# Mixture-of-experts stage: weighted inputs from transposed activations and spread routing weights, in place of transposes of weighted inputs

## The chip, the cores and the metric

The kernel runs on one core of a Trainium2 chip. The metric is the device time of one launch in microseconds. The five instruction streams of the core that matter here are PE (TensorE, matrix multiplies), DVE (VectorE), ACT (ScalarE), POOL (GpSimd) and SP (which here only issues DMAs).

## The reference

Sixteen sequences of 256 tokens with 128 channels pass through four blocks, each followed by a layer norm: a state-space block, a mixture of experts, a second state-space block, and a transformer of six layers. All data are float32. The change is in the mixture of experts only:

```
def _moe_linear(x, router_w, expert_w):      # 8 experts, top 2
    logits = x @ router_w.T
    vals, idx = top_k(logits, 2)
    combine = sum over k of softmax(vals)[k] * onehot(idx[k])    # [tokens, 8]
    return sum over e of combine[:, e:e+1] * (x @ expert_w[e].T)
g = _moe_linear(x, router_gate, w_gate)      # 128 -> 512
u = _moe_linear(x, router_up,   w_up)        # 128 -> 512
d = _moe_linear(silu(g) * u, router_down, w_down)   # 512 -> 128
```

`combine` has two nonzero entries in a row, but the kernel computes all eight experts for every token and multiplies by the weights. For `g` and `u` it puts the weight on the input: `combine[t, e] * x[t, :]` is made first, for 8 experts of `g` and 8 of `u`, and the eight products are summed in PSUM.

## The kernel before

The work is four phases, one after another: `ssm_phase`, `moe_phase`, `ssm2_phase`, `transformer_phase`. `X` (all sequences, tokens on partitions, in two halves `t` of 128) stays in SBUF between them.

`moe_phase` (L489) runs 17 passes written out in a loop (`passes`, L535). Pass n does the routing part R of sequence n beside the expert part M of sequence m = n-1. The order on each engine is the order of the code; there is no planner, and semaphores alone tie the engines together (`Steps` counts the steps of a sequence on each engine).

- **PE**, in a pass (L716 to L730): `r_xt` transposes x of sequence n (two 128x128 blocks); `m_experts(0, ..)` is the gate product of sequence m (L689, 4 column chunks of 8 experts, into `pg`); `r_lg` the router logits; `m_experts(1, ..)` the up product into `pu`; between its four chunks, `r_ct` transposes the 16 weighted inputs `xc` of sequence n (two blocks each, 32 transposes, L672); `m_ld` the logits of the down router; `m_down(0)` and `m_down(1)` the down product (L713).
- **DVE**: the top-2 of sequence n (`top2`, L544), the 32 products x times weight into `xc` (L584, tokens on partitions, so that a weight is one value a partition), then for sequence m `it` = silu(g) * u (L590), the second top-2, the weighted sums of the down product (L600, eight for each half t), and the layer norm.
- **ACT**: the copy of the transposed x to `xT` (L620), exponentials, silu of `pg` (L629), and 16 copies of the transposed weighted inputs from PSUM to `xcT` (L633), which the gate and up products of the next pass read. `xcT` has two buffers.
- **POOL and SP** do nothing in this phase. All loads of the phase's weights were issued in the phase before (L133).

Waits that matter: `r_ct` waits for `xc` (L668) and, from the third on, for ACT's copy two before (L670), because there are two PSUM banks for it; `m_ld` waits for `it` and for ACT's last copy (L697, L699), since it writes the same bank; the gate product waits for all copies of its sequence (L682).

Of the kernel before, what the change touches and what calls it, by code (L numbers as in the profile page):

```python
# [20 lines left out]
ALU = mybir.AluOpType  # L21
# [467 lines left out]
def moe_phase(nc, I, X, ident, experts):  # L489
# [3 lines left out]
    with ctx:  # L493
        wg, wu, wd = experts.wg, experts.wu, experts.wd
        rgu, rd, iota = experts.rgu, experts.rd, experts.iota
        xT = sb("b_xT", [P, L])
        lg = sb("b_lg", [P, 3 * T, NE])
        mx = sb("b_mx", [P, 3 * T, 8])
        ix = sb("b_ix", [P, 3 * T, 8], U32)
# [5 lines left out]
        oh = sb("b_oh", [P, 3 * T, NE])  # L505
        o2 = sb("b_o2", [P, 3 * T, NE])
        cb = sb("b_cb", [P, 3 * T, NE])
        xc = sb("b_xc", [P, T, 2 * NE, D])
        xcT = [sb(f"b_xcT{i}", [P, 2 * NE, L]) for i in range(2)]
        sig = sb("b_sig", [P, CF * L])  # L510
        it = sb("b_it", [P, CF, L])
# [12 lines left out]
        loaded, LOADS = experts.loaded, experts.LOADS  # L524

        route = "mx*{0} ix*{0} xf df sm p0 p1 oh*{0} o2*{0} cb"
        pr_ = Steps(ctx, nc, "b_pe_r", f"xt lg ct*{2 * NE}")
        vr = Steps(ctx, nc, "b_dve_r", "lc " + route.format(2 * T) + f" xc*{T * 2 * NE}")
        ar = Steps(ctx, nc, "b_act_r", f"xT ex ctc*{2 * NE}")
        pm_ = Steps(ctx, nc, "b_pe_m", "g*2 u ld d0 d1")  # L530
        vm = Steps(ctx, nc, "b_dve_m", "gu lc " + route.format(T) + f" acc0*{NE} acc1*{NE} bn*2 ag*2 ve nw*{VRS} out*2")
        am_ = Steps(ctx, nc, "b_act_m", "sig*2 ex")
# [2 lines left out]
        def passes(run, eng):  # L535

            for n in range(NSEQ + 1):
                run((n, n % 2) if n < NSEQ else None, (n - 1, (n - 1) % 2) if n else None)

        @block.vector  # L540
        def _(e):
            e.wait_ge(loaded, 16 * LOADS)

            def top2(st, act, n, a, b):  # L544
# [26 lines left out]
                e.tensor_tensor(cb[:, a:b, :], oh[:, a:b, :], o2[:, a:b, :], ALU.add).then_inc(st.sem, 1)  # L571
                e.wait_ge(st.sem, st.at("cb", n))

            def run(R, M):
                if R:
                    n, p = R
                    e.wait_ge(pr_.sem, pr_.at("lg", n))
                    e.tensor_copy(lg[:, 0:2 * T, :], pm[1][:, 0:2 * T * NE].rearrange("p (j n) -> p j n", n=NE))\
                        .then_inc(vr.sem, 1)
                    top2(vr, ar, n, 0, 2 * T)  # L580
                    for x in range(2 * NE):
                        for t in range(T):
                            j = 2 * t + x // NE
                            e.tensor_scalar(xc[:, t, x, :], X[:, n, t, :], cb[:, j, x % NE:x % NE + 1],  # L584
                                            None, ALU.mult).then_inc(vr.sem, 1)
                if M:
                    m, p = M
                    e.wait_ge(am_.sem, am_.at("sig", m))
                    e.wait_ge(pm_.sem, pm_.at("u", m))
                    e.tensor_tensor(it[:, :, :].rearrange("p c l -> p (c l)"), pu[:, :], sig[:, :], ALU.mult).then_inc(vm.sem, 1)  # L590
                    e.wait_ge(pm_.sem, pm_.at("ld", m))
                    e.tensor_copy(lg[:, 2 * T:3 * T, :], pm[1][:, 0:T * NE].rearrange("p (j n) -> p j n", n=NE))\
                        .then_inc(vm.sem, 1)
                    top2(vm, am_, m, 2 * T, 3 * T)
                    for t in range(T):
                        e.wait_ge(pm_.sem, pm_.at(f"d{t}", m))
                        for x in range(NE):
                            if x:
                                e.wait_ge(vm.sem, vm.at(f"acc{t}", m, NE - x))
                            e.scalar_tensor_tensor(acc[:, t, :], pdown[t][:, x * D:(x + 1) * D], cb[:, 2 * T + t, x:x + 1],  # L600
                                                   acc[:, t, :] if x else X[:, m, t, :],
                                                   ALU.mult, ALU.add).then_inc(vm.sem, 1)
                    e.wait_ge(vm.sem, vm.at("acc1", m))
                    layernorm_stats(e, vm, m, lambda t: acc[:, t, :], stats, mv, "")
                    e.wait_ge(vm.sem, vm.at("ag", m))
                    e.tensor_scalar(ve[:, :], mv[:, :, 1], EPS, None, ALU.add).then_inc(vm.sem, 1)
                    vector_rsqrt(e, vm, m, "nw", y[:, :], ve[:, :], h[:, :], tt[:, :])
                    e.wait_ge(vm.sem, vm.at("nw", m))
                    for t in range(T):
                        e.tensor_scalar(X[:, m, t, :], acc[:, t, :], mv[:, t, 0:1], y[:, t:t + 1], ALU.subtract, ALU.mult)\  # L610
                            .then_inc(vm.sem, 1)
            passes(run, e)

        @block.scalar
        def _(e):
            def run(R, M):
                if R:
                    n, p = R
                    e.wait_ge(pr_.sem, pr_.at("xt", n))
                    e.activation(xT[:, :], pm[0][:, 0:L], ACT.Copy).then_inc(ar.sem, 1)  # L620
                    e.wait_ge(vr.sem, vr.at("df", n))
                    e.activation(ex[:, 0:2 * T], df[:, 0:2 * T], ACT.Exp).then_inc(ar.sem, 1)
                if M:
                    m, q = M
                    for j in range(2):
                        e.wait_ge(pm_.sem, pm_.at("g", m, 1 - j))
                        if j == 0 and later(m):
                            e.wait_ge(vm.sem, vm.at("gu", m - 1))
                        e.activation(sig[:, j * 512:(j + 1) * 512], pg[:, j * 512:(j + 1) * 512], ACT.Silu).then_inc(am_.sem, 1)  # L629
                if R:  # L630
                    for x in range(2 * NE):
                        e.wait_ge(pr_.sem, pr_.at("ct", n, 2 * NE - 1 - x))
                        e.activation(xcT[p][:, x, :], pm[x % 2][:, 0:L], ACT.Copy).then_inc(ar.sem, 1)  # L633
                if M:
                    e.wait_ge(vm.sem, vm.at("df", m))
                    e.activation(ex[:, 2 * T:3 * T], df[:, 2 * T:3 * T], ACT.Exp).then_inc(am_.sem, 1)
            passes(run, e)

        @block.tensor
        def _(e):  # L640
            e.wait_ge(loaded, 16 * LOADS)

            def run(R, M):
# [9 lines left out]
                def r_lg():  # L653
                    if R:
                        n, p = R
                        e.wait_ge(ar.sem, ar.at("xT", n))
                        if n >= 2:
                            e.wait_ge(vm.sem, vm.at("lc", n - 2))
                        for t in range(T):
                            m = e.matmul(pm[1][:, t * 2 * NE:(t + 1) * 2 * NE], xT[:, t * P:(t + 1) * P], rgu[:, :],  # L660
                                         start=True, stop=True)
                        m.then_inc(pr_.sem, 1)

                def r_ct(a, b):
                    if R:
                        n, p = R
                        for x in range(a, b):
                            e.wait_ge(vr.sem, vr.at("xc", n, T * (2 * NE - 1 - x)))  # L668
                            if x >= 2:
                                e.wait_ge(ar.sem, ar.at("ctc", n, 2 * NE + 1 - x))  # L670
                            for t in range(T):
                                m = e.transpose(pm[x % 2][:, t * P:(t + 1) * P], xc[:, t, x, :], ident[:, :])  # L672
                            m.then_inc(pr_.sem, 1)

                def m_experts(r, a, b):

                    if M:
                        m, p = M
                        w, o = ((wg, pg), (wu, pu))[r]
                        if a == 0:  # L680
                            if r == 0:
                                e.wait_ge(ar.sem, ar.at("ctc", m))  # L682
                                if later(m):
                                    e.wait_ge(vm.sem, vm.at("acc0", m - 1))
                            elif later(m):
                                e.wait_ge(vm.sem, vm.at("gu", m - 1))
                        for j in range(a, b):
                            for x in range(NE):
                                last = e.matmul(o[:, j * L:(j + 1) * L], w[:, x, j * P:(j + 1) * P], xcT[p][:, r * NE + x, :],  # L689
# [4 lines left out]
                def m_ld():  # L694
                    if M:
                        m, p = M
                        e.wait_ge(vm.sem, vm.at("gu", m))  # L697
                        if R:
                            e.wait_ge(ar.sem, ar.at("ctc", R[0]))  # L699
                        for t in range(T):  # L700
                            for j in range(CF):
                                last = e.matmul(pm[1][:, t * NE:(t + 1) * NE], it[:, j, t * P:(t + 1) * P], rd[:, j, :],
                                                start=j == 0, stop=j == CF - 1)
                        last.then_inc(pm_.sem, 1)
# [9 lines left out]
                                                wd[:, j, b * 512:(b + 1) * 512], start=j == 0, stop=j == CF - 1)  # L714
                        last.then_inc(pm_.sem, 1)
                r_xt()  # L716
                m_experts(0, 0, 2)
                r_lg()
                m_experts(0, 2, 4)
                m_experts(1, 0, 1)  # L720
                r_ct(0, 4)
                m_experts(1, 1, 2)
                r_ct(4, 8)
                m_experts(1, 2, 3)
                r_ct(8, 12)
                m_experts(1, 3, 4)
                r_ct(12, 16)
                m_ld()
                m_down(0)
                m_down(1)  # L730
# [1046 lines left out]
```

## Time and profile before

| | us |
|---|---|
| median of 3 runs (4464.75 to 4467.26) | 4465.24 |
| profiled execution, its own time | 4472.1 |
| its span, first to last instruction | 4470.2 |
| mixed passes of the expert phase, 110.09 to 896.01 | 785.92 |
| one of them (268.42 to 318.93) | 50.51 |

The span is the distance from the first to the last instruction on the core; the profiled execution's own time is 1.9 us longer. The granted TensorE clock is a share of 2.4 GHz, 0.97 over the whole span. "Idle before" in brackets is how long the engine had nothing to do before that instruction, and what it was waiting for.

### The profile page before, as it was taken

Reading aid. Unit: us, or ns where it says so; the run is one execution under the profiler, and the core shown is the slowest. Engines: PE = TensorE matmul, PEld = TensorE weight load, DVE = VectorE, ACT = ScalarE, POOL = GpSimd, SP = SyncE. Lnnn points to the kernel's source line nnn. Section 1 sums busy time; section 2 is a strip of 40 time slices with the busy share of each in tenths; the row PEclk is TensorE's granted clock in tenths of the full one; section 3 lists DMA queues with packets and bytes.
Section 4 is the critical chain, followed back from the end, with each engine's and each line's share of the span. In section 5 each row is a group of like instructions: output and inputs, shape, how many; then the busy total and the mean of one; then the engine's idle time right before and its main releaser. Section 6 shows DMA issues by size and latency. Waiting matters only on the chain.

```text
span 4470.2 us, 146512 instructions
## 1 busy us (share of the span) xinstructions
PE 4226.6 (95%) x64231; PEld 3077.6 (69%) x64231; DVE 3363.1 (75%) x7591; ACT 2458.3 (55%) x4522; POOL 2133.5 (48%) x1317
## 2 busy tenths in 40 slices
PE   5999999988699999999999999999999999998997
PEld 3777776666377777777777777777777777766665
DVE  5444444444698898888988888888888889887784
ACT  2111111111367676776776776767767767666663
POOL 1000000001466666666666666666666666665552
PEclk8999999999799999999999999999999999999998
DMA  3000000000011111111111111111111111111110
GB/s 128 1 1 1 1 1 1 1 1 1 23 40 39 34 50 54 39 36 39 53 50 35 40 39 48 50 39 39 42 51 45 39 34 49 54 37 37 34 34 24
DMA packets 70594, 152.46 MB, mean 34 GB/s; under 512 B 14524, under 2 KB 43079, under 8 KB 69575
## 3 DMA queue, kind: packets, MB, share of 16 engines
q1 hardware_dynamic: 69958, 143.09, 10.8%
q8 instruction: 509, 8.34, 0.8%
q14 instruction: 127, 1.03, 0.1%
HBM read 27.69 MB, written 2.10 MB: 7 GB/s over the span
## 4 chain that ended last, share of the span: by engine, by line
PE 63%; DVE 4%; ACT 3%; issue 3%; POOL 2%; POOLq 0%; DVEq 0%
PE pQ L1537 14%; PE pS L1521 9%; PE pM L1603 7%; PE pO L1581 6%; PE pM L1592 6%; PE pC L1637 5%; PE pO L1568 4%; PE pT L1568 4%; PE pT L1549 3%; PE pC L1647 3%; ACT sq L1406 2%; POOL rot L1166 1%; POOL rot L1174 1%; ACT pS L1390 1%; DVE rot L1256 1%
## 5 line engine op out<-in xcount | busy, mean ns | idle before, releaser
L1174 POOL TENSOR_TENSOR rot<-rot,m 128x1024 f32<-128x1024 f32 x384 | 905.1, 2357 | 397.3 <-DVE m L1260 397.3
L1166 POOL TENSOR_TENSOR rot<-rot,rn 128x1024 f32<-128x1024 f32 x384 | 732.8, 1908 | 245.9 <-DVE rn L102 245.9
L1406 ACT ACTIVATE sq<-pQ 128x1024 f32<-128x1024 f32 x384 | 393.7, 1025 | 463.1 <-PE pQ L1537 463.1
L1183 POOL TENSOR_TENSOR E<-E,rc 128x512 f32<-128x512 f32 x384 | 400.5, 1043 | 352.4 <-DVE rc L1246 352.1
L1256 DVE TENSOR_TENSOR rot<-pQ,tabl 128x1024 f32<-128x1024 f32 x384 | 461.8, 1203 | 36.0 <-ACT sq L1406 35.4
L1568 PEld LDWEIGHTS pO<-PT,V 64*64 64x64 f32 x12288 | 389.9, 135 | 132.8 <-issue 124.1
L1521 PEld LDWEIGHTS pS<-kT,qT 64*32 64x32 f32 x24576 | 369.6, 108 | 141.3 <-issue 105.3
L1260 DVE TENSOR_TENSOR m<-pQ,tabl 128x1024 f32<-128x1024 f32 x384 | 466.2, 1214 | 0.0
L1271 DVE TENSOR_REDUCE n<-sq 128x16 f32<-128x1024 f32 x384 | 464.1, 1209 | 0.0
L1568 PE MATMUL pO<-PT,V 64*64 64x32 f32 x12288 | 432.0, 221 | 29.7 <-issue 27.3
L1521 PE MATMUL pS<-kT,qT 64*32 64x64 f32 x24576 | 434.6, 220 | 22.9 <-issue 12.6
L1592 PE MATMUL pM<-ident,rot 128*128 128x128 f32 x3072 | 422.2, 281 | 23.8 <-POOL rot L1166 23.8
L786 POOL MEMSET c_xn<- 128x48 f32 x1 | 0.1, 147 | 926.6 <-POOLq L493 926.6
L1568 PE MATMUL pT<-PT,V 64*64 64x32 f32 x12288 | 434.7, 221 | 0.0
L1537 PE MATMUL pQ<-wq,xs 128*128 128x512 f32 x768 | 385.9, 625 | 10.5 <-DVE m L1260 9.1
L1568 PEld LDWEIGHTS pT<-PT,V 64*64 64x64 f32 x12288 | 392.1, 133 | 0.0
L1537 PE MATMUL pQ<-wk,xs 128*128 128x512 f32 x768 | 364.9, 598 | 9.0 <-DVE m L1260 9.0
L1592 PEld LDWEIGHTS pM<-ident,rot 128*128 128x128 f32 x3072 | 337.5, 142 | 46.3 <-POOL rot L1166 29.3
L1603 PE MATMUL pM<-wv,xs 128*128 128x512 f32 x768 | 365.1, 598 | 0.0
L1581 PE MATMUL pO<-oT,wo 128*128 128x256 f32 x1536 | 348.6, 380 | 0.6 <-ACT oT L1421 0.4
L1232 DVE TENSOR_REDUCE mx<-pS 128x8 f32<-128x512 f32 x384 | 262.7, 684 | 82.8 <-PE pS L1521 82.6
L1581 PEld LDWEIGHTS pO<-oT,wo 128*128 128x128 f32 x1536 | 285.1, 191 | 36.6 <-ACT oT L1421 1.2
(221 smaller groups left out, 7842.2 us busy)
## 6 DMA issues: line engine op xcount, KB each, us to landing
V<-V SPq DMA_DIRECT2D x192, 384.0 KB, 3.5
xs<-XT SPq DMA_DIRECT2D x192, 64.0 KB, 2.9
V<-V SPq DMA_DIRECT2D x96, 128.0 KB, 3.3
ys<-XT SPq DMA_DIRECT2D x192, 64.0 KB, 2.1
wq<-in_wqkv SPq DMA_DIRECT2D x6, 512.0 KB, 4.8
wk<-in_wqkv SPq DMA_DIRECT2D x6, 512.0 KB, 4.0
wv<-in_wqkv SPq DMA_DIRECT2D x6, 512.0 KB, 5.5
wo<-in_wo SPq DMA_DIRECT2D x6, 512.0 KB, 3.9
```

The costliest lines, as they stand in the source:

```text
L1166: e.tensor_tensor(r, r, rn[b % 2][:, c:c + HEADS].unsqueeze(2).to_broadcast([P, HEADS, HD]), ALU.mult)\
L1174: e.tensor_tensor(rot[j % RING][:, :], rot[j % RING][:, :], m2[:, :, :].rearrange("p h d -> p (h d)"), ALU.add)\
L1256: e.tensor_tensor(rot[j % RING][:, :].rearrange("p (h d) -> p h d", d=HD), pQ[:, :].rearrange("p (h d) -> p h d", d=HD), tl[:, t, 2 * w, : ...
L1260: e.tensor_tensor(m2[:, :, :].rearrange("p h (b d) -> p h b d", b=2), pQ[:, :].rearrange("p (h b d) -> p h b d", b=2, d=HD // 2)[:, :, ::- ...
L1271: e.tensor_reduce(n2[:, c:c + HEADS], sq[:, :].rearrange("p (h d) -> p h d", d=HD), AX.X, ALU.add)\
L1406: e.activation(sq[:, :], pQ[:, :], ACT.Square).then_inc(a_sq.sem, 1)
L1521: x = e.matmul(pS[32 * j:32 * j + 32, b * KEYS:(b + 1) * KEYS], q[r:r + HD, h // 2, WIN * w:WIN * (w + 1)], k[r:r + HD, h // 2, WIN * w:WI ...
L1537: x = e.matmul(pQ[:, i * 512:(i + 1) * 512], xs[n % 3][:, t * P:(t + 1) * P], wqkv[w][:, i * 512:(i + 1) * 512], start=True, stop=True)
L1568: x = e.matmul(pOV[b % 2][c:c + HD, j // 2, w // 4, WIN * (w % 2):WIN * (w % 2 + 1)], V[n % 2][r:r + KEYS, w // 4, 1 - w % 2, h * HD:(h + ...
L1581: x = e.matmul(pO[:, 0:L], wo[:, c, :], oT[:, c, :], start=c == 0, stop=c == N // P - 1)
L1592: x = e.transpose(pM[i][:, c * P:(c + 1) * P], rot[j % RING][:, (4 * i + c) * P:(4 * i + c + 1) * P], ident[:, :])
L1603: e.matmul(pM[i][:, :], xs[n % 3][:, t * P:(t + 1) * P], wqkv[2][:, i * 512:(i + 1) * 512], start=True, stop=True)\
```

## The change

The weighted inputs are made directly in the transposed layout (channels on partitions, tokens along the row). There a weight varies along the row, so that it has to be present on all 128 partitions.

- PE transposes the routing weights `cb` of the two token halves (two transposes, output 16 partitions x 256) in place of the 32 transposes of `xc`. `r_ct` takes its only place between the up chunks 1 and 2; `r_lg` moves ahead by one gate chunk. `m_ld` no longer waits for ACT's copies of sequence n.
- ACT copies that result once to `cT` (16 partitions, a row is one expert's weights over 256 tokens) in place of 16 copies.
- SP, for each of the 16 rows, issues a DMA that reads this row of 1 KB from its one partition of `cT` and writes it to all 128 partitions of `cB` (128 KB written a DMA, 2 MB a sequence). `cB` has one buffer: the DMAs wait for both of its readers of the sequence before.
- DVE multiplies `cB[:, 0:8]` by `xT` in one instruction of 128 x 2048 (step `xg`, gate half), after the sums of half 0 of sequence m; the 32 products at L584 are gone.
- POOL multiplies `cB[:, 8:16]` by `xT` in one instruction of the same size (step `xu`, up half).
- The gate product waits for `xg`, the up product for `xu`. `xT` has two buffers.

```diff
-        xT = sb("b_xT", [P, L])
+        xT = [sb(f"b_xT{i}", [P, L]) for i in range(2)]
+        cT = sb("b_cT", [2 * NE, L])
+        cB = sb("b_cB", [P, 2 * NE, L])
...
-        xc = sb("b_xc", [P, T, 2 * NE, D])
...
+        @block.sync
+        def _(e):
+            for n in range(NSEQ):
+                e.wait_ge(ar.sem, ar.at("ctc", n))
+                if n:
+                    e.wait_ge(vr.sem, vr.at("xg", n - 1))
+                    e.wait_ge(gr.sem, gr.at("xu", n - 1))
+                for x in range(2 * NE):
+                    e.dma_start(cB[:, x, :], cT[x:x + 1, :].unsqueeze(1).to_broadcast([1, P, L])).then_inc(wide[x // NE], 16)
+
+        @block.gpsimd
+        def _(e):
+            for n in range(NSEQ):
+                p = n % 2
+                if n >= 2:
+                    e.wait_ge(pm_.sem, pm_.at("u", n - 2))
+                e.wait_ge(ar.sem, ar.at("xT", n))
+                e.wait_ge(wide[1], 16 * NE * (n + 1))
+                e.tensor_tensor(xcT[p][:, NE:2 * NE, :], cB[:, NE:2 * NE, :], xT[p][:, :].unsqueeze(1).to_broadcast([P, NE, L]), ALU.mult)\
+                    .then_inc(gr.sem, 1)
...
-                    for x in range(2 * NE):
-                        for t in range(T):
-                            j = 2 * t + x // NE
-                            e.tensor_scalar(xc[:, t, x, :], X[:, n, t, :], cb[:, j, x % NE:x % NE + 1],
-                                            None, ALU.mult).then_inc(vr.sem, 1)
...
+                    summed(m, 0)
+                if R:
+                    n, p = R
+                    e.wait_ge(wide[0], 16 * NE * (n + 1))
+                    e.tensor_tensor(xcT[p][:, 0:NE, :], cB[:, 0:NE, :], xT[p][:, :].unsqueeze(1).to_broadcast([P, NE, L]), ALU.mult)\
+                        .then_inc(vr.sem, 1)
+                if M:
+                    summed(m, 1)
...
-                    for x in range(2 * NE):
-                        e.wait_ge(pr_.sem, pr_.at("ct", n, 2 * NE - 1 - x))
-                        e.activation(xcT[p][:, x, :], pm[x % 2][:, 0:L], ACT.Copy).then_inc(ar.sem, 1)
+                    e.wait_ge(pr_.sem, pr_.at("ct", n))
+                    if n:
+                        e.wait_ge(vr.sem, vr.at("xg", n - 1))
+                        e.wait_ge(gr.sem, gr.at("xu", n - 1))
+                    e.activation(cT[:, :], pm[0][0:2 * NE, 0:L], ACT.Copy).then_inc(ar.sem, 1)
...
-                        for x in range(a, b):
-                            e.wait_ge(vr.sem, vr.at("xc", n, T * (2 * NE - 1 - x)))
-                            if x >= 2:
-                                e.wait_ge(ar.sem, ar.at("ctc", n, 2 * NE + 1 - x))
-                            for t in range(T):
-                                m = e.transpose(pm[x % 2][:, t * P:(t + 1) * P], xc[:, t, x, :], ident[:, :])
-                            m.then_inc(pr_.sem, 1)
+                        e.wait_ge(vr.sem, vr.at("cb", n))
+                        for t in range(T):
+                            m = e.transpose(pm[0][0:2 * NE, t * P:(t + 1) * P], cb[:, 2 * t:2 * t + 2, :].rearrange("p j n -> p (j n)"),
+                                            ident[:, :])
+                        m.then_inc(pr_.sem, 1)
...
                             if r == 0:
-                                e.wait_ge(ar.sem, ar.at("ctc", m))
+                                e.wait_ge(vr.sem, vr.at("xg", m))
...
+                                e.wait_ge(gr.sem, gr.at("xu", m))
...
-                        if R:
-                            e.wait_ge(ar.sem, ar.at("ctc", R[0]))
...
                 r_xt()
-                m_experts(0, 0, 2)
+                m_experts(0, 0, 1)
                 r_lg()
-                m_experts(0, 2, 4)
-                m_experts(1, 0, 1)
-                r_ct(0, 4)
-                m_experts(1, 1, 2)
-                r_ct(4, 8)
-                m_experts(1, 2, 3)
-                r_ct(8, 12)
-                m_experts(1, 3, 4)
-                r_ct(12, 16)
+                m_experts(0, 1, 4)
+                m_experts(1, 0, 2)
+                r_ct()
+                m_experts(1, 2, 4)
                 m_ld()
```

## Rows read from the trace of the kernel before

**Rows 1.** The page's second part: the span in 40 slices of 111.8 us
```profile
PE   5999999988699999999999999999999999998997
PEclk8999999999799999999999999999999999999998
GB/s 128 1 1 1 1 1 1 1 1 1 23 40 39 34 50 54 39 36 39 53 50 35 40 39 48 50 39 39 42 51 45 39 34 49 54 37 37 34 34 24
```

**Rows 2.** Timeline of PE, one mixed pass: start, duration, engine, line, [idle before]
```profile
268.42 0.38 PE L650 MATMUL b_pm<-ident,X 128*128 128x128 f32 x2
...
282.90 3.62 PE L689 MATMUL b_pu<-b_xcT,b_wu 128*128 128x256 f32 x16
286.36 0.60 PE L672 MATMUL b_pm<-ident,b_xc 128*128 128x128 f32 x4
287.30 0.69 PE L672 MATMUL b_pm<-ident,b_xc 128*128 128x128 f32 x4 [0.35 <-ACT b_xcT L633]
287.82 3.62 PE L689 MATMUL b_pu<-b_xcT,b_wu 128*128 128x256 f32 x16
...
297.68 3.62 PE L689 MATMUL b_pu<-b_xcT,b_wu 128*128 128x256 f32 x16
301.13 0.60 PE L672 MATMUL b_pm<-ident,b_xc 128*128 128x128 f32 x4
302.08 0.69 PE L672 MATMUL b_pm<-ident,b_xc 128*128 128x128 f32 x4 [0.35 <-ACT b_xcT L633]
303.33 1.92 PE L702 MATMUL b_pm<-b_rd,b_it 128*128 128x8 f32 x16 [0.57 <-ACT b_xcT L633]
305.11 7.11 PE L713 MATMUL b_pg<-b_wd,b_it 128*128 128x512 f32 x16
312.06 7.03 PE L713 MATMUL b_pd<-b_wd,b_it 128*128 128x512 f32 x16
318.93 0.38 PE L650 MATMUL b_pm<-ident,X 128*128 128x128 f32 x2
```

**Rows 3.** Windows, all mixed passes: length, busy by engine, PEclk, DMA share, GB/s
```profile
110.09:896.01 785.92, 756.63 (x3210) 552.80 (x3211) 337.42 (x1653) 148.66 (x346) 0.00 (x0) 0.96 0.00 1
```

**Rows 4.** Timeline of PE, the last pass, which has no routing part
```profile
910.25 13.98 PE L689 MATMUL b_pu<-b_xcT,b_wu 128*128 128x256 f32 x64
925.61 1.95 PE L702 MATMUL b_pm<-b_rd,b_it 128*128 128x8 f32 x16 [1.39 <-DVE b_it L590]
```

**Rows 5.** Timeline of the first pass, which has no expert part
```profile
92.60 0.66 PE L650 MATMUL b_pm<-ident,X 128*128 128x128 f32 x2 [9.19 <-PEq L244]
99.14 0.19 DVE L571 TENSOR_TENSOR b_cb<-b_oh,b_o 128x32 f32<-128x32 f32 x1
99.91 9.71 PE L672 MATMUL b_pm<-ident,b_xc 128*128 128x128 f32 x32 [5.14 <-DVE b_xc L584]
110.09 0.44 PE L650 MATMUL b_pm<-ident,X 128*128 128x128 f32 x2 [0.47 <-ACT b_xcT L633]
```

**Rows 6.** Windows: the loads of the first phase, then a pair of SBUF-to-SBUF copies
```profile
20.00:30.00 10.00, 8.59 (x50) 5.41 (x50) 2.08 (x7) 1.20 (x2) 2.11 (x4) 0.88 0.99 415
2031.25:2033.50 2.25, 2.25 (x14) 1.98 (x13) 2.22 (x3) 1.23 (x1) 1.79 (x1) 1.00 0.78 233
2032.75:2033.50 0.75, 0.75 (x7) 0.69 (x6) 0.72 (x2) 0.00 (x0) 0.75 (x1) 1.00 0.56 202
```

**Rows 7.** Timeline of SP's queue, the issues of those copies (384 and 128 KB)
```profile
2030.23 0.54 SPq L1125 DMA_DIRECT2D V<-V  x1
2030.81 0.60 SPq L1126 DMA_DIRECT2D V<-V  x1
```

**Rows 8.** Groups of instructions: busy us, mean ns of one, idle before
```profile
L1174 POOL TENSOR_TENSOR rot<-rot,m 128x1024 f32<-128x1024 f32 x384 | 905.1, 2357 | 397.3 <-DVE m L1260 397.3
L1183 POOL TENSOR_TENSOR E<-E,rc 128x512 f32<-128x512 f32 x384 | 400.5, 1043 | 352.4 <-DVE rc L1246 352.1
L590 DVE TENSOR_TENSOR b_it<-b_pu,b_sig 128x1024 f32<-128x1024 f32 x16 | 19.6, 1224 | 237.7 <-PE b_pu L689 237.7
```

**Rows 9.** Timeline of PE: the same 32 multiplies after an idle stretch, and warm
```profile
71.34 5.69 PE L465 MATMUL a_pu<-a_xpad,a_fused 128*64 128x256 f32 x32
...
38.81 3.68 PE L465 MATMUL a_pu<-a_xpad,a_fused 128*64 128x256 f32 x32
```

**Rows 10.** Windows around that idle stretch: PEclk is the third number from the end
```profile
70.00:74.00 4.00, 3.81 (x22) 2.45 (x24) 3.00 (x14) 1.43 (x4) 0.00 (x0) 0.50 0.02 4
74.00:78.00 4.00, 3.68 (x30) 2.12 (x26) 2.39 (x6) 0.76 (x3) 0.00 (x0) 0.82 0.00 0
```

**Rows 11.** Timeline of DVE at the end of that mixed pass
```profile
312.34 0.35 DVE L600 SCALAR_TENSOR_TENSOR b_acc<-b_pg,b_cb,X 128x128 f32<-128x128 f32 x1 [3.83 <-PE b_pg L713]
312.73 2.67 DVE L600 SCALAR_TENSOR_TENSOR b_acc<-b_pg,b_cb,b_acc 128x128 f32<-128x128 f32 x7
```

More of the change, by code:

```diff
@@ L526, in moe_phase @@
         route = "mx*{0} ix*{0} xf df sm p0 p1 oh*{0} o2*{0} cb"
-        pr_ = Steps(ctx, nc, "b_pe_r", f"xt lg ct*{2 * NE}")
-        vr = Steps(ctx, nc, "b_dve_r", "lc " + route.format(2 * T) + f" xc*{T * 2 * NE}")
-        ar = Steps(ctx, nc, "b_act_r", f"xT ex ctc*{2 * NE}")
+        pr_ = Steps(ctx, nc, "b_pe_r", "xt lg ct")
+        vr = Steps(ctx, nc, "b_dve_r", "lc " + route.format(2 * T) + " xg")
+        ar = Steps(ctx, nc, "b_act_r", "xT ex ctc")
+        gr = Steps(ctx, nc, "b_pool_r", "xu")
+        wide = [ctx.enter_context(nc.semaphore(f"b_wide_{k}")) for k in "gu"]
         pm_ = Steps(ctx, nc, "b_pe_m", "g*2 u ld d0 d1")
@@ L572, in top2, with summed @@
                 e.wait_ge(st.sem, st.at("cb", n))
+            def summed(m, t):
+                e.wait_ge(pm_.sem, pm_.at(f"d{t}", m))
+                for x in range(NE):
+                    if x:
+                        e.wait_ge(vm.sem, vm.at(f"acc{t}", m, NE - x))
+                    e.scalar_tensor_tensor(acc[:, t, :], pdown[t][:, x * D:(x + 1) * D], cb[:, 2 * T + t, x:x + 1],
+                                           acc[:, t, :] if x else X[:, m, t, :],
+                                           ALU.mult, ALU.add).then_inc(vm.sem, 1)
             def run(R, M):
@@ L594, in run @@
                     top2(vm, am_, m, 2 * T, 3 * T)
-                    for t in range(T):
[L596 to L602, printed above, removed]
+                    summed(m, 0)
[6 more added lines that the diff above has]
+                    summed(m, 1)
                     e.wait_ge(vm.sem, vm.at("acc1", m))
@@ L619, in run @@
                     e.wait_ge(pr_.sem, pr_.at("xt", n))
-                    e.activation(xT[:, :], pm[0][:, 0:L], ACT.Copy).then_inc(ar.sem, 1)
+                    if n >= 2:
+                        e.wait_ge(gr.sem, gr.at("xu", n - 2))
+                    e.activation(xT[p][:, :], pm[0][:, 0:L], ACT.Copy).then_inc(ar.sem, 1)
                     e.wait_ge(vr.sem, vr.at("df", n))
@@ L659, in r_lg, with r_ct @@
                         for t in range(T):
-                            m = e.matmul(pm[1][:, t * 2 * NE:(t + 1) * 2 * NE], xT[:, t * P:(t + 1) * P], rgu[:, :],
+                            m = e.matmul(pm[1][:, t * 2 * NE:(t + 1) * 2 * NE], xT[p][:, t * P:(t + 1) * P], rgu[:, :],
                                          start=True, stop=True)
                         m.then_inc(pr_.sem, 1)
-                def r_ct(a, b):
+                def r_ct():
                     if R:
                         n, p = R
-                        for x in range(a, b):
-                            e.wait_ge(vr.sem, vr.at("xc", n, T * (2 * NE - 1 - x)))
-                            if x >= 2:
-                                e.wait_ge(ar.sem, ar.at("ctc", n, 2 * NE + 1 - x))
-                            for t in range(T):
-                                m = e.transpose(pm[x % 2][:, t * P:(t + 1) * P], xc[:, t, x, :], ident[:, :])
-                            m.then_inc(pr_.sem, 1)
+                        e.wait_ge(vr.sem, vr.at("cb", n))
[3 more added lines that the diff above has]
+                        m.then_inc(pr_.sem, 1)
                 def m_experts(r, a, b):
@@ L681, in m_experts @@
                             if r == 0:
-                                e.wait_ge(ar.sem, ar.at("ctc", m))
+                                e.wait_ge(vr.sem, vr.at("xg", m))
                                 if later(m):
                                     e.wait_ge(vm.sem, vm.at("acc0", m - 1))
-                            elif later(m):
-                                e.wait_ge(vm.sem, vm.at("gu", m - 1))
+                            else:
+                                e.wait_ge(gr.sem, gr.at("xu", m))
+                                if later(m):
+                                    e.wait_ge(vm.sem, vm.at("gu", m - 1))
                         for j in range(a, b):
```

## The prediction, made before the result was known

> **What bounds the kernel now.** I read the slices of the span first, because the change touches one phase. The expert phase begins at 92.6 us and ends near 950, slices 1 to 8; there PE is busy nine tenths or more of nearly every slice, at a clock of nine tenths or more, and the DMA queues move 1 GB/s [rows 1]. So the phase is PE's, with every DMA engine free. The other phases are not touched.
>
> Then the PE timeline of one mixed pass. It lasts 318.93 - 268.42 = 50.51 us, and PE has no gap over 0.6 us in it; the small gaps are at the transposes, where PE waits for ACT's copies [rows 2]. All fifteen mixed passes take 785.92 us, 52.4 each, since in some the granted clock falls for a short stretch (0.96 on average) [rows 3]. Whatever leaves PE's stream in a mixed pass shortens it, until another chain is longer than what is left. That chain is the question here, for the change builds a new one, through SP and the DMA engines, where nothing ran before.
>
> **What is removed.** Each of the three inner groups of 8 transposes costs PE the distance to the next up chunk, 287.82 - 286.36 = 1.46 us (three groups: 4.4) [rows 2]. The fourth is followed by `m_ld`: from the end of the up product (297.68 + 3.62 = 301.30) to the down router at 303.33 are 2.03 us; in the last pass, where no transposes stand there, the same distance is 925.61 - (910.25 + 13.98) = 1.38 us, ended by DVE's `it` [rows 2, 4]. The fourth group is therefore worth only 0.65 us, because `it` is late next. The two new transposes cost about what `r_xt`'s two do, 0.3 us (busy 0.38, partly pipelined) [rows 2]. Net on PE: 4.4 + 0.65 - 0.3 = 4.75 us a mixed pass, 71 us over fifteen. ACT's 16 copies and DVE's 32 products go too; neither engine was the bound, so this earns nothing beyond the gaps counted.
>
> **What is added, in order of the chain for one sequence.**
> - ACT's one copy to `cT`: about 0.4 us. With the two transposes and the hand-overs, 1.1 us from the end of up chunk 1 to `cT` ready.
> - SP issues 16 DMAs. An issue of this kind takes 0.54 to 0.60 us, so 16 take 9 us [rows 7]; the data of the first flow about 1.0 us after issue starts (issue at 2030.23, bytes from 2031.25) [rows 6, 7]. SP has nothing else to do in this phase, so nothing is queued behind.
> - The DMAs move 16 x 131,072 bytes = 2.10 MB. Call their duration D.
> - POOL's `xu`, 128 x 2048. No such row exists; 128 x 512 takes 1.04 us and 128 x 1024 up to 2.36 us [rows 8], so between 4 x 1.04 = 4.2 and 2 x 2.36 = 4.7 us. I take 4.2, and 0.8 for the landing and the semaphores on either side. POOL has no other work, so nothing stands behind its wait.
> - PE's up chunks 0 and 1 (6.9 us at full clock, twice the 3.4 that separate 282.90 from 286.36) [rows 2]. `r_ct` stands behind them in program order, so that the weights of sequence n+1 cannot be transposed before `xu` of sequence n is done. `cB` has one buffer, and its DMAs wait for the same `xu` anyway.
> - DVE's `xg`: 2 x 1.22 = 2.4 us [rows 8]. It stands between the two sums of the down product. Each sum takes 3.0 us (0.35 and 2.67) [rows 11], and the second's input comes 7.0 us after the first's (a down half on PE) [rows 2]. So `xg` is hidden if the gate rows have landed by then; if not, the second sum, the layer norm and the top-2 of the next sequence wait behind it. The gate rows are the first half of D, and PE's next gate product waits for `xg` as well.
>
> The cycle from one `cT` to the next is therefore 1.0 + D + 0.8 + 4.2 + 6.9 + 1.1 = D + 14 us. With D under about 30 us it hides behind the remaining 45.8 us of PE work of a pass. Everything rests on D.
>
> **D.** The trace shows no DMA that reads one partition. All 16 engines together move 415 GB/s when they spread over 128 partitions, 26 GB/s each [rows 6]. The quickest case is that reading one partition 128 times is no slower: 2.10 MB at 415 GB/s are 5 us, at the 233 GB/s of the SBUF-to-SBUF pair 9 us, the same as SP's issues [rows 6, 7]. The slowest is that a partition gives no more than the rows show for one: the end of that pair, L1126, which reads 32 partitions by the code, runs at 202 GB/s, or 6.3 GB/s a partition, which makes D 333 us [rows 6]. In between lies one lane's rate: if all 16 engines have to draw from the one place where the row lies, they share what the trace shows one engine to move, 26 GB/s. A DMA then takes 131,072 / 25.9 GB/s = 5.06 us and D is 81 us. I take this value. In every fast row the bytes go to or from many partitions at once; here sixteen engines want the same 1 KB, row after row, and a source that all of them share has not been seen to give more than one of them takes. It is also the value of the three that lies nearest to a row in kind: a rate of one path, not of all and not of a guess per partition.
>
> The Trainium skill speaks against this change at the same place: by "SBUF — State Buffer", section "Door 1: The DMA port swizzle", DMA bandwidth depends on how many of the 16 SBUF ports a transfer's partitions reach, about 27.2 GB/s a port, with partitions 0 to 3 on one port. By its figure (an estimate) a row would take 4.8 us, D would be 77 us and the time some 64 us below my forecast. Its table speaks of tiles at both ends' width and not of a repeated source row; no row of this trace shows it.
>
> **The sum with D = 81 us.** PE now idles some 25 us a pass before the up product. After such an idle stretch the clock stands at 0.50, the 1.2 GHz level, and comes back within the next window [rows 10]; 32 multiplies that take 3.68 us warm took 5.69 there [rows 9], so 2.0 us more a resumption. The cycle is 81 + 14 + 2 = 97 us. In the first pass `cb` is ready at 99.33; two transposes at the low clock (0.66) and the copy put `cT` at 100.7 [rows 5]. The fifteenth cycle later is 100.7 + 15 x 97 = 1555.7; DMAs and `xu` of sequence 15 add 87, and the last pass's up product starts at 1642.7 in place of 910.25 [rows 4]. With 2 us for the cold start the rest moves by 1642.7 - 910.25 + 2 = +735 us; written for any D, with D + 16 a cycle, it is 15 (D + 16) + D + 6 + 100.7 - 910.25 + 2, or 16 D - 561. Against the profiled execution's own 4472.1 us that is 5207; the runs' median lies 6.9 us lower, so 5200 us.
>
> **The rivals.**
> - *The source row is no bottleneck.* D is 5 to 30 us, the chain hides, and PE keeps the 4.75 us a pass. In the first pass, DVE and PE reach 110 us as before (`cT` at 100.7, 1.0 to the first data, eight issues 4.5, landing 0.8: 107; `xg` 2.4). 4472.1 - 71 = 4401 on the profile, 4394 on the median; 4380 to 4420 with the clock's short falls going either way. For it: idle queues, rows of 1 KB, 16 engines, 415 GB/s seen. Against it: never seen from one partition. It decides from D = 35 us (16 D = 561), 60 GB/s, twice and a third what one engine's share is.
> - *Half a bottleneck.* The rows overlap at two or more places and run at 33 to 60 GB/s: D 35 to 63, time 4465 to 4910. The 16 rows lie on consecutive partitions and the DMAs are started in order, so I see little to spread them.
> - *Worse than one lane.* Sixteen readers in each other's way, or a single partition giving less: 20 GB/s makes D 105 and 5584 us, the 6.3 GB/s above 9230 us.
> - *The change doesn't take PE's transposes away.* Excluded by the diff; they are gone from the stream.
>
> **How the numbers follow.** Forecast (D 63 to 97 us, 4910 to 5450): 0.55. Worse than that: 0.12. Half a bottleneck: 0.06. Source row no bottleneck: 0.25. Landing within 0.2% of before by a D near 35: 0.02. A difference of 0.2% (9 us) is about what a measurement of this kernel can tell from none. So faster 0.25, same 0.02, slower 0.73. The forecast's own range is 4910 to 5450 us. As the fast case has more than 2 in 10, the range must reach it: 4380 to 5450, which leaves the 0.12 above outside.
>
> **What would show it.** Right: SP's queue with 16 issues a pass and the DMA busy share high for some 80 us each time; `xu` starting 83 us after `cT`; PE waiting for POOL before the up product 25 us a pass and for DVE before the gate product; granted clock 0.5 after each; the L672 rows down from 512 to 32; a phase of 1580 us. Wrong: if the rows land within 15 us of issue and PE's pass lasts 46 us, the source row was no bottleneck; if the share is high and D well over 100 us, one partition gives less than one lane.

## The result, and the profile after

| | before | changed |
|---|---|---|
| median of 3 runs, us | 4465.24 | 5042.53 (5038.19 to 5044.11) |
| span of the profiled execution, us | 4470.2 | 5040.7 |
| ratio, 95% interval | | 1.129 (1.1271 to 1.1309) |

The change costs 577 us. The time lies inside the stated range and on the side that was forecast; the forecast itself, 5200, was 158 us too high.

The second part of the page of the changed kernel, in slices of 126 us:

```profile
PE   4565555556567699999999999999999999999997
PEclk7777777778779899999999999999999999999998
DMA  4757565766640011111111111111111111111110
GB/s 119 27 22 27 22 26 23 26 24 24 26 17 1 12 39 36 39 49 49 40 36 47 49 40 40 40 52 41 40 40 52 44 36 40 50 46 39 35 36 23
```

The expert phase now fills slices 1 to 11. PE is busy half of it, where it was busy nine tenths and more [rows 1]; the 16 DMA engines are busy some six tenths of it and yet move only 22 to 27 GB/s in all slices but the last. In the first phase of before, engines with a busy share of 0.99 moved 415 GB/s [rows 6], so here most of the busy time must be waiting inside the transfers.

One pass on PE, and the POOL products of two sequences:

```profile
560.23 0.38 PE L682 MATMUL b_pm<-ident,X 128*128 128x128 f32 x2
574.97 5.99 PE L721 MATMUL b_pg<-b_xcT,b_wg 128*128 128x256 f32 x16 [14.36 <-DVE b_xcT L627]
...
581.17 10.61 PE L721 MATMUL b_pg<-b_xcT,b_wg 128*128 128x256 f32 x48
609.99 9.01 PE L721 MATMUL b_pu<-b_xcT,b_wu 128*128 128x256 f32 x32 [18.21 <-POOL b_xcT L561]
618.84 0.38 PE L701 MATMUL b_pm<-ident,b_cb 128*16 128x128 f32 x2
619.05 7.07 PE L721 MATMUL b_pu<-b_xcT,b_wu 128*128 128x256 f32 x32
627.54 1.95 PE L732 MATMUL b_pm<-b_rd,b_it 128*128 128x8 f32 x16 [1.42 <-DVE b_it L618]
```
```profile
605.44 4.50 POOL L561 TENSOR_TENSOR b_xcT<-b_cB,b_xT 128x2048 f32<-128x2048 f32 x1 [82.73 <-DMA b_cB<-b_cT]
691.81 4.49 POOL L561 TENSOR_TENSOR b_xcT<-b_cB,b_xT 128x2048 f32<-128x2048 f32 x1 [81.88 <-DMA b_cB<-b_cT]
```

PE's 32 transposes are gone, and two long waits stand in their place: 14.4 us for `xg`, DVE's product of weights and inputs for the gate half, and 18.2 us for `xu`, POOL's product for the up half. Both in turn wait for DMAs. A pass lasts 86.4 us here (691.81 - 605.44), 86.8 on average over the phase, in place of 50.5 in the pass shown before and 52.4 on average [rows 2, 3]. The distance from the end of the up product to the down router, ended by `it`, is 1.42 us, close to the 1.39 of the last pass of before [rows 4].

The DMAs by tile, durations in ns of issue (least, median, most) and the time to landing:

```profile
L551 SPq DMA_DIRECT2D b_cB<-b_cT x256: 469/4912/4949, 99.8 to 1458.2; - x128
DMA to landing us min/median/max: 6.9/15.9/17.9
```

An issue took 0.54 to 0.60 us before [rows 7]. Here the median is 4.91 us, and a DMA lands 15.9 us after its issue, so that about three (15.9 / 4.91) are under way at a time. I read this as a full queue: SP can put in a DMA only when one leaves. Then a DMA of 131,072 bytes takes 4.91 us, which is 26.7 GB/s. In one-microsecond windows of the first sequence, with one of 70 us at the end (third to last number: clock; then the busy share of the DMA engines; last: GB/s):

```profile
119.00:120.00 1.00, 0.00 (x0) 0.00 (x0) 0.00 (x0) 0.00 (x0) 0.00 (x0) 0.50 0.81 26
120.00:121.00 1.00, 0.00 (x0) 0.00 (x0) 0.00 (x0) 0.00 (x0) 0.00 (x0) 0.50 0.99 83
121.00:122.00 1.00, 0.00 (x0) 0.00 (x0) 0.00 (x0) 0.00 (x0) 0.00 (x0) 0.50 0.77 25
...
138.00:139.00 1.00, 0.00 (x0) 0.00 (x0) 0.00 (x0) 0.00 (x0) 0.00 (x0) 0.50 0.80 74
139.00:140.00 1.00, 0.00 (x0) 0.00 (x0) 0.84 (x1) 0.00 (x0) 0.00 (x0) 0.50 0.90 29
...
153.00:154.00 1.00, 1.00 (x6) 0.90 (x5) 0.00 (x0) 0.00 (x0) 0.00 (x0) 1.00 0.70 84
...
101.00:171.00 70.00, 16.79 (x68) 14.15 (x68) 6.10 (x28) 2.69 (x4) 0.00 (x0) 0.62 0.81 30
```

The rate stays between 20 and 31 GB/s, except near 120 us, from 133 to 139 us and from 153 to 156 us. Counted at 4.9 us a row from 101, these are the fourth, the eighth and (after what the first two saved) the twelfth row. Something changes every four rows. 2.10 MB take 70 us.

### The profile page after: what moved, and what is told of

It is laid out like the page before. It is cut to its first block, busy times and chain, and to the rows that moved or that the text cites. A ratio compares the mean times of both kernels' runs of the same rounds, so it can differ in the third digit from the quotient of the medians.

```text
span 5040.7 us, 144925 instructions
## 1 busy us (share of the span) xinstructions
PE 4228.1 (84%) x63751; PEld 3072.6 (61%) x63751; DVE 3295.6 (65%) x7095; ACT 2380.3 (47%) x4282; POOL 2207.6 (44%) x1333
## 4 chain that ended last, share of the span: by engine, by line
PE 56%; DVE 3%; issue 3%; ACT 3%; POOL 2%; POOLq 0%; DVEq 0%
PE pQ L1562 13%; PE pS L1546 8%; PE pM L1628 6%; PE pM L1617 6%; PE pO L1606 6%; PE pC L1662 5%; PE pO L1593 4%; PE pT L1593 3%; PE pT L1574 3%; PE pC L1672 2%; ACT sq L1431 2%; POOL rot L1191 1%; POOL rot L1199 1%; DVE rot L1281 1%; ACT pS L1415 1%
## 5 line engine op out<-in xcount | busy, mean ns | idle before, releaser
L561 POOL TENSOR_TENSOR b_xcT<-b_cB,b_xT 128x2048 f32<-128x2048 f32 x16 | 71.9, 4495 | 1383.6 <-DMA b_cB<-b_cT 1383.6
L721 PE MATMUL b_pu<-b_xcT,b_wu 128*128 128x256 f32 x1024 | 264.3, 423 | 297.1 <-POOL b_xcT L561 297.1
L721 PE MATMUL b_pg<-b_xcT,b_wg 128*128 128x256 f32 x1024 | 261.3, 420 | 283.3 <-DVE b_xcT L627 283.3
L618 DVE TENSOR_TENSOR b_it<-b_pu,b_sig 128x1024 f32<-128x1024 f32 x16 | 19.6, 1224 | 654.3 <-PE b_pu L721 654.3
L721 PEld LDWEIGHTS b_pu<-b_xcT,b_wu 128*128 128x128 f32 x1024 | 218.1, 216 | 339.3 <-POOL b_xcT L561 303.6
L721 PEld LDWEIGHTS b_pg<-b_xcT,b_wg 128*128 128x128 f32 x1024 | 215.2, 213 | 322.0 <-DVE b_xcT L627 287.9
## 6 DMA issues: line engine op xcount, KB each, us to landing
b_cB<-b_cT SPq DMA_DIRECT2D x256, 128.0 KB, 15.9
```

## The experiments

Theory A: all engines draw a row from one place of SBUF, that place gives 26 to 27 GB/s, and four adjacent partitions share it. Theory B: a DMA of 128 rows of 1 KB from SBUF to SBUF costs this much whatever it reads. Theory C: the limit is the single partition. The times of the changed kernel, wide source and through HBM are medians of 3, 4 and 4 executions; each of the others is one execution, so that I read no difference of a few microseconds from them. "Landed" is from the first issue of sequence 0 to the start of its POOL product, the cycle is the mean distance of the 16 POOL products.

| kernel | landed, us | cycle, us | time, us |
|---|---|---|---|
| changed | 72.2 | 86.8 | 5042.5 |
| wide source | 11.8 | 46.1 | 4386.0 |
| rows spread | 40.7 | 54.9 | 4530.8 |
| rows in two places | 79.4 | 94.0 | 5153.0 |
| half rows | 36.9 | 49.7 | 4446.5 |
| through HBM | 9.0 | 46.1 | 4387.1 |
| early, two buffers | 72.2 | 66.6 | 4739.1 |
| two queues | 41.0 | 69.3 | 4746.9 |
| order alone | 44.0 | 58.1 | 4578.7 |
| spread and two queues | 30.4 | 49.6 | 4441.3 |

**Wide source.** The same DMAs, with another source. ACT's copy to `xT` besides waits for the `xg` of two sequences before.

```diff
-                    e.dma_start(cB[:, x, :], cT[x:x + 1, :].unsqueeze(1).to_broadcast([1, P, L])).then_inc(wide[x // NE], 16)
+                    e.dma_start(cB[:, x, :], xT[n % 2][:, :]).then_inc(wide[x // NE], 16)
```

> Each of the 16 DMAs reads a tile of 128 partitions (the sequence's transposed activations, xT) in place of one row of cT; size, count, order, targets and waits stay. The spread weights are left out by this, so the weighted inputs are not the reference's. Theory A (all engines draw from one place of SBUF, which gives 26 to 27 GB/s; changed kernel: D of 72 us from the first issue to the POOL product, 87 us a pass): D falls to 9 to 12 us, SP's issues, the chain hides, a pass is 46 us and the time 4380 to 4410 us. Theory B (128 rows of 1 KB between SBUF and SBUF cost 4.4 to 4.9 us a DMA whatever they read): D stays 72 and the time 5040. This run also measures what the removed transposes are worth when the chain is hidden: I said 71 us.

Measured: 4386.04 us, ratio to before 0.9821 (0.9798 to 0.9843). Issues and rate:

```profile
L551 SPq DMA_DIRECT2D b_cB<-b_xT x256: 464/601/1578, 98.2 to 799.0; - x128
```
```profile
100.00:108.00 8.00, 0.82 (x2) 0.73 (x3) 2.29 (x1) 0.00 (x0) 0.00 (x0) 0.50 0.62 207
```

An issue takes 0.60 us again and the rate is 207 GB/s, about SP's pace of one 128 KB DMA every 0.6 us. The targets, sizes and counts are those of the changed kernel, so theory B falls: what costs is what the DMA reads. It also shows that everything else in the change is hidden or gains.

**Rows spread, rows in two places.** Both make a zeroed tile `cw` with DVE copies of the weights at chosen columns, so that the transposes put the rows on chosen partitions; DMA x then reads that partition. In two places, the gate rows lie on 0 to 3 and 32 to 35 and the up rows on 4 to 7 and 36 to 39. The spread layout:

```diff
+                        e.tensor_copy(cw[:, t, :].rearrange("p (j x s) -> p j x s", j=2, s=4)[:, :, 0:NE, 0], cb[:, 2 * t:2 * t + 2, :]).then_inc(vr.sem, 1)
...
-                    e.dma_start(cB[:, x, :], cT[x:x + 1, :].unsqueeze(1).to_broadcast([1, P, L])).then_inc(wide[x // NE], 16)
+                    e.dma_start(cB[:, x, :], cT[64 * (x // NE) + 4 * (x % NE):64 * (x // NE) + 4 * (x % NE) + 1, :].unsqueeze(1).to_broadcast([1, P, L])).then_inc(wide[x // NE], 16)
```

> The 16 rows of cT lie 4 partitions apart: gate rows on partitions 0, 4, ..., 28, up rows on 64, 68, ..., 92 (two DVE copies into a zeroed tile ahead of the two transposes, otherwise the same work). In the changed kernel the rate leaves 26 to 29 GB/s only near rows 4, 8 and 12 (83 GB/s in one microsecond). Theory A, with four adjacent partitions sharing one place: now every row is at a boundary; a row alone takes 4.9 us, 16 take 79, the three boundaries of the changed kernel saved 7, so 2.4 to 2.8 each; 15 of them give D of 36 to 43 us and 4470 to 4590 us. Theory B (cost per DMA): 5040. Theory C (each partition by itself is the limit, so that neighbours already differ): 5040, and the bursts stay near every fourth row.

> The gate rows lie on partitions 0 to 3 and 32 to 35, the up rows on 4 to 7 and 36 to 39; work as in the spread layout otherwise. By the Trainium skill, SBUF — State Buffer, section Door 1, partitions 32 apart are on the same port. If that is so (A with that map) only row 8 is at a boundary: D of 76 us, 5090 to 5120 us, and no burst at rows 4 and 12. If only neighbours share a place (A without that map), bursts at rows 4, 8 and 12 as before and 5040. B and C: 5040.

Measured: spread 4530.8 us, as A expected; in two places 5153.0 us, 33 us above the upper end of A with that map and 110 above the changed kernel. That the one change of place left saved so little there I did not take apart. Windows of the spread kernel, then of the one with two places:

```profile
110.00:120.00 10.00, 0.00 (x0) 0.00 (x0) 0.00 (x0) 0.00 (x0) 0.00 (x0) 0.50 0.82 59
120.00:130.00 10.00, 5.64 (x18) 4.65 (x19) 2.29 (x1) 0.00 (x0) 0.00 (x0) 0.58 0.86 58
```
```profile
120.00:122.00 2.00, 0.00 (x0) 0.00 (x0) 0.00 (x0) 0.00 (x0) 0.00 (x0) 0.50 0.78 25
140.00:142.00 2.00, 0.00 (x0) 0.00 (x0) 0.10 (x1) 0.00 (x0) 0.00 (x0) 0.50 0.82 52
152.00:154.00 2.00, 2.00 (x11) 1.77 (x10) 1.49 (x15) 0.86 (x2) 0.00 (x0) 1.00 0.87 28
```

With each row 4 partitions from the last, the rate is 58 to 59 GB/s from 110 to 130 us. With rows 4 to 7 put 32 partitions above rows 0 to 3, the burst at 120 us is gone, as is the one at the twelfth row; only the one at the eighth, near 140, is left. So the place is shared by four neighbours and, for the partitions tried, by the four that lie 32 above, and theory C falls. The Trainium skill, "SBUF — State Buffer", section "Door 1: The DMA port swizzle", has this map and 27.2 GB/s a port; the traces agree with the map for the partitions tried in this way (0 to 15 and 32 to 39) and, at 26.7 GB/s of reading from one place, nearly with the figure.

**Half rows.**

```diff
-                    e.dma_start(cB[:, x, :], cT[x:x + 1, :].unsqueeze(1).to_broadcast([1, P, L])).then_inc(wide[x // NE], 16)
+                    e.dma_start(cB[:, x, 0:P], cT[x:x + 1, 0:P].unsqueeze(1).to_broadcast([1, P, P])).then_inc(wide[x // NE], 16)
```

> Each DMA moves only the first 128 of 256 tokens of its row (512 bytes to each partition, 64 KB a DMA); the weights of the other tokens are left at zero, so the output differs. 16 DMAs and 128 rows each as before. Theory A: D halves to 36 us, and by 16 us of time for each us of D the time falls by 570 to about 4470 to 4490 us. Theory B, a cost per DMA or per row of it: D stays near 72, time near 5040.

Measured: 4446.5 us, landed in 36.9 us for 72.2. The price goes with the bytes, as A has it, not with the number of DMAs. The time is 24 us below A's range. The cold starts go too, since PE waits 1.4 us or nothing before the up product:

```profile
439.47 7.17 PE L726 MATMUL b_pu<-b_xcT,b_wu 128*128 128x256 f32 x32 [1.43 <-POOL b_xcT L564]
446.48 0.38 PE L706 MATMUL b_pm<-ident,b_cb 128*16 128x128 f32 x2
```

From the start of the up product to the transposes are 7.0 us, where the changed kernel takes 8.85; over fifteen passes that is about 28 us, which A's range had left out.

**Through HBM.** HBM is the memory outside the core; 16 KB go out to it, then two DMAs of 1 MB come in.

```diff
+                e.dma_start(scr[n % 2].rearrange("o x l -> (o x) l"), cT[:, :]).then_inc(staged, 16)
+                e.wait_ge(staged, 16 * (n + 1))
+                for r in range(2):
+                    e.dma_start(cB[:, r * NE:(r + 1) * NE, :], scr[n % 2][:, r * NE:(r + 1) * NE, :].to_broadcast([P, NE, L])).then_inc(wide[r], 16)
```

> SP writes cT (16 KB) to a scratch tensor in HBM, waits for it, and two DMAs of 1 MB spread 8 rows each from there to all partitions. The same result as the changed kernel. Theory A (the limit is the place in SBUF that the row lies in): D is 2 us for the write, 2 to 3 for the first read, 5 to 9 for 2 MB, in all 10 to 14 us; the chain hides and the time is 4380 to 4420 us. Rival (the same bytes read by all engines are slow wherever they lie): D stays at tens of us, time 4600 or more.

Measured: 4387.10 us, ratio to before 0.9827 (0.9811 to 0.9843): 1.7% faster than before, a small gain but clear of the noise, and far faster than the changed kernel, with its computation. It has landed in 9.0 us, a little sooner than the 10 to 14 expected. Its DMAs (KB each, us to landing), the window of sequence 0, and a pass on PE:

```profile
b_cB<-b_scr SPq DMA_DIRECT2D x32, 1024.0 KB, 6.2
b_scr<-b_cT SPq DMA_DIRECT2D x16, 16.0 KB, 1.4
```
```profile
100.00:107.00 7.00, 0.00 (x0) 0.00 (x0) 2.23 (x1) 0.00 (x0) 0.00 (x0) 0.50 0.81 300
```
```profile
438.80 0.38 PE L686 MATMUL b_pm<-ident,X 128*128 128x128 f32 x2
...
460.19 0.38 PE L705 MATMUL b_pm<-ident,b_cb 128*16 128x128 f32 x2
460.40 7.07 PE L725 MATMUL b_pu<-b_xcT,b_wu 128*128 128x256 f32 x32
468.89 1.95 PE L736 MATMUL b_pm<-b_rd,b_it 128*128 128x8 f32 x16 [1.42 <-DVE b_it L622]
...
484.52 0.38 PE L686 MATMUL b_pm<-ident,X 128*128 128x128 f32 x2
```

The same 16 KB are repeated 128 times from HBM at 300 GB/s over 7 us, start included. Count and size of the DMAs differ too from the changed kernel; that these are not the cause rests on the wide source, which kept both. A pass is 484.52 - 438.80 = 45.72 us, 4.79 less than the 50.51 of before [rows 2].

**Early transposes, two buffers.** `cB` and `cT` doubled, and in PE's order:

```diff
-                m_experts(1, 0, 2)
                 r_ct()
-                m_experts(1, 2, 4)
+                m_experts(1, 0, 4)
```

> cB and cT get a second buffer and the two transposes of the weights stand before the up product, so that the DMAs of sequence n+1 no longer wait for the POOL product and two up chunks of sequence n. The DMAs stay as they are. If the cycle is D plus 14 us as predicted, the queue now never runs dry, a pass is 70 to 74 us in place of 87, and the time falls by about 200 to 4800 to 4870 us. Rival (the 14 us were not on the path, or the next transposes are held by the gate rows): no change, 5040.

Measured: 4739.1 us, a cycle of 66.6. So the 14 us were on the path. But the gain is 303 us, not 200, and the time is 61 us below my range. A queue that never runs dry also overlaps the last row of one sequence with the first of the next, which lie in different places. A cycle late in the phase has four bursts about 17 us apart, the fourth at the change of sequence (the POOL product starts at 506.0):

```profile
453.00:454.00 1.00, 1.00 (x7) 0.87 (x6) 0.00 (x0) 0.00 (x0) 0.00 (x0) 1.00 0.67 70
470.00:471.00 1.00, 1.00 (x4) 0.38 (x3) 0.93 (x3) 0.00 (x0) 0.00 (x0) 1.00 0.69 74
487.00:488.00 1.00, 1.00 (x6) 0.90 (x5) 0.63 (x4) 0.05 (x1) 0.00 (x0) 1.00 0.74 95
504.00:505.00 1.00, 0.00 (x0) 0.00 (x0) 0.00 (x0) 0.00 (x0) 0.00 (x0) 0.50 0.64 74
```

2.10 MB in 66.6 us are 31.5 GB/s, against 30 within one sequence of the changed kernel.

**Two queues.** The up rows are issued by ACT after its last exponential of the pass (`for x in range(NE, 2 * NE)` moved there), the gate rows by SP.

> The 8 up rows are issued by ACT on its own queue, after its exponential, while SP issues the 8 gate rows; both read cT as in the changed kernel, at partitions 8 to 15 and 0 to 7. Theory A: two places are read at a time, 50 to 55 GB/s together, D of 40 us and about 4530 us (4470 to 4650; ACT's later work waits behind its issues). Rival D (the engines themselves are held at 26 GB/s in all by this kind of DMA): D stays 72, 5040.

Measured: 4746.9 us, about 100 above A's range; all rows of sequence 0 landed in 41.0 us, as A expected, at 51 to 65 GB/s in windows of 10 us from 110 us on. PE and ACT in a later pass:

```profile
486.76 6.24 PE L725 MATMUL b_pg<-b_xcT,b_wg 128*128 128x256 f32 x16 [19.77 <-DVE b_xcT L627]
...
510.55 0.38 PE L705 MATMUL b_pm<-ident,b_cb 128*16 128x128 f32 x2
```
```profile
442.70 0.37 ACT L665 ACTIVATE b_cT<-b_pm 16x256 f32<-16x256 f32 x1 [6.53 <-PE b_pm L705]
...
454.28 33.42 ACTq L672 DMA_DIRECT2D b_cB<-b_cT  x8
487.81 0.39 ACT L650 ACTIVATE b_xT<-b_pm 128x256 f32<-128x256 f32 x1 [33.33 <-issue]
```

Two places at a time, as A has it, held; my step from D to the time did not. The eight gate rows still take about 39 us from their two places, one after the other (8 x 4.9), and they have a chain of their own: `cT` at 443.07, the gate product from 486.76, then up chunks 0 and 1, the transposes at 510.55 and the next `cT` some 25 us after the start of the gate product, together 68 us. In the changed kernel the up rows' chain (86.8) hid this one. ACT besides sat 33 us in its eight issues, with `xT` behind them.

**Order alone, spread with two queues.** The first is the changed kernel with one line:

```diff
-                for x in range(2 * NE):
+                for x in (0, 4, 1, 5, 2, 6, 3, 7, 8, 12, 9, 13, 10, 14, 11, 15):
```

> The changed kernel with one edit: SP issues the rows in the order 0, 4, 1, 5, 2, 6, 3, 7, then 8, 12, 9, 13, 10, 14, 11, 15, so that neighbours in the queue come from different groups of four partitions. Same layout, same DMAs, same bytes. Theory A (four adjacent partitions share a place with 27 GB/s; transfers from two places overlap in one queue): as with the spread rows, 56 to 60 GB/s, D of about 41 us, a pass of 55 us, 4520 to 4550 us. Rival (the gain of the spread rows came from their distance over the whole of SBUF, or from the 128-partition layout of cT): less than half of it, 4750 or more.

> The spread rows, with the 8 up rows issued by ACT on its own queue. One queue with spread rows ran at 56 to 60 GB/s (two places' worth), two queues with rows in place at 53. If each queue can draw on two places and the engines are free for more, 90 to 110 GB/s flow while both queues have rows; gate rows 22 us, up rows 11 us later and as long, a pass of 48 to 51 us and 4440 to 4510 us. Rival (the engines hold no more than this for rows whose source is contended): 55 to 60 GB/s in all, and with ACT's xT copy behind its issues 4530 us or more.

Measured: order alone 4578.7 us, landed in 44.0 us. Nine tenths of what spreading gained comes from the order in the queue, with the layout untouched; the rest (52 to 56 GB/s in windows of 10 us from 110 us on, where the spread rows had 58 to 59, and 29 us above my range) I did not take apart. Spread with two queues: 4441.3 us, inside its range, and while both queues have rows the rate is

```profile
106.00:114.00 8.00, 0.00 (x0) 0.00 (x0) 0.00 (x0) 0.00 (x0) 0.00 (x0) 0.50 0.77 93
```

So the engines were not the limit: in units of 26.7 GB/s, one queue with spread rows draws on about two places at a time (58), two such queues on three to four (93). Why a queue overlaps two transfers and no more is open.

## Why the prediction was right, and where its size was off

- **PE is the bound, the other engines are not; what leaves PE shortens the pass.** Right, and seen where the chain is hidden: 4.79 us a pass (through HBM), where I had 4.75; 76.7 us in all between medians (4463.8 and 4387.1), where I had 71. Of the difference, the first pass gives about 3: the gate product waits there for DVE's product, which ends at 107.1 (first row, through HBM), where it started at 110.4 before (second row); some 2 us are left open.

```profile
104.77 2.29 DVE L631 TENSOR_TENSOR b_xcT<-b_cB,b_xT 128x2048 f32<-128x2048 f32 x1 [7.58 <-DMA b_cB<-b_scr]
```
```profile
110.37 7.07 PE L689 MATMUL b_pg<-b_xcT,b_wg 128*128 128x256 f32 x32
```

- **The chain `cT`, DMAs, `xu`, up chunks, transposes sets the cycle.** Right. The cycle less the landing (the two middle columns of the table) is 14.1 to 14.6 us in all four kernels that have the whole chain on the path (changed, rows spread, two places, order alone), though the landing goes from 40.7 to 79.4. "Landed" holds D and the 1.0 and 0.8 us around it, so this is to be compared with my 4.2 + 6.9 + 2.0 + 1.1 = 14.2. Between spread and two places the time rises by 622.2 us for 38.7 us of landing, 16.1 each, where I had 16. Step by step in the changed kernel: POOL 4.50 (I had 4.2), up chunks 609.99 to 618.84 = 8.85 with the cold start (8.9), transposes and copy 0.8 (1.1).
- **D = 81 us: the mis-sized term.** The single row is nearly as priced, 4.91 us against 5.06, which is 2.4 us of the 11. But I put all 16 one after another at that rate, and they are so only within a place. At each change of place two transfers overlap, and the three changes leave 70 us in place of 78.6. With D = 70 the formula 16 D - 561 gives +559 us, and with POOL's 0.3 more a pass +564; the spans differ by 570.5. So 16 x 11 = 176 us too much came from this term, and the smaller terms together hid some 11 of them (the forecast change of the profile was 735, 165 above the 570.5). I had written that with consecutive partitions "I see little to spread them"; the rows lay in four places, not one. The rival *Half a bottleneck* (D 35 to 63, chance 0.06) named this overlap; it is there, but weaker than the rival's 33 GB/s, so that D fell into the forecast's own range.
- **Idle of 25 us a pass before the up product.** It is 18.2 in the pass shown, plus 14.4 before the gate product, a wait which I had named without a price; the latter isn't on the cycle, since the gate product ends at 591.8 and the POOL product at 609.9. The clock fell to 0.50 in the gaps, as said: the first gate chunk took 5.99 us, where the same 16 records take 3.62 warm [rows 2].
- **The chances.** The rival "the source row is no bottleneck", at 0.25, was wrong on the row, but its time was right for a source that is none: with the source elsewhere the time is 4386 and 4387, against its 4394. My own range, 4910 to 5450, held the time by itself, so the hit does not rest on the low end of the stated range, which was there for that rival.

## What to carry to other kernels

Price a DMA by how many places of SBUF it reads from, not only by how many engines it runs on (writing to few places was not tried here). To spread something small over all partitions, pass it through HBM. Reordering the queue, so that neighbours come from different places, gets back most of the loss but not all: it left the kernel at 4578.7 us, above the 4465 of before. Look at the issue time in the queue: it was 0.4 to 0.6 us in the two kernels whose rows landed quickly, and 4.9 us where the queue was full. And when work moves off the bound engine, write down the whole loop that the moved work closes, from its input of one iteration to the next: here the 5 us saved on PE were real, and a loop of D + 14 us, with 2 more for the cold start, became longer than the pass.

## What the runs showed of the hardware

- A row of 1 KB on one partition, written to 128 by 16 engines, is read at 26.7 GB/s in all; the same bytes from HBM went at 300 GB/s over 7 us, and from 128 partitions at SP's pace, 207.
- Partitions 0 to 3 share that rate, and so do each next four up to 15 (bursts at every fourth row). With 0 to 3 go 32 to 35, and with 4 to 7 go 36 to 39 (the bursts at the fourth and twelfth row are gone when rows are placed so).
- Where neighbouring rows lie in different places, one queue reaches 58 GB/s and two queues 93. The engines' busy share is 0.81 at 30 GB/s from one row after another and 0.81 at 300 GB/s from HBM, so the share alone says nothing on what is moved.
- A full queue holds up the engine that issues: 33 us on ACT for eight DMAs.
- POOL's product of 128 x 2048 takes 4.50 us and DVE's 2.29, the former between the bounds from smaller rows (4.2 to 4.7).
